# Moving the shared expert's sum, row numbers and a normalization between the engines of a macaron transformer block

## What is computed

```python
# x: (16, 512, 128), 8192 tokens; D = 128, 8 experts of 384, shared expert of 128, 16 heads of 8
def ffn(x):
    normed = (x - mu) * rsqrt(var + eps) * gamma + beta
    probs  = softmax(normed @ router_w.T);  top_v, top_i = top_k(probs, 2);  gates = softmax(top_v)
    out = sum over e of comb[:, e] * swiglu(normed, gate_up_w[e], down_w[e])
    return out + swiglu(normed, shared_gate_up_w, shared_down_w)
x = x + 0.5 * ffn(layernorm(x))
x = x + attention(layernorm(x))        # with relative-position terms
x = x + 0.5 * ffn(layernorm(x))
```

## Time and profile before

| | us |
|---|---|
| median of 3 runs (2189.92 to 2193.46) | 2190.85 |
| profiled execution | 2192.66 |
| its span | 2190.5 |

### The profile page before, as it was taken

How to read it: one execution, slowest core, us unless ns; L and a number is a source line. 1 busy time by engine, 2 the same in 40 slices (tenths; PEclk the granted TensorE clock), 3 DMA queues, 4 the chain that set the end, 5 groups by cost and what they waited for, 6 DMA issues and landing times. The chain is left out here.

```text
span 2190.5 us, 64350 instructions
## 1 busy us (share of the span) xinstructions
PE 2028.2 (93%) x22952; PEld 1233.5 (56%) x22953; DVE 1925.1 (88%) x4201; ACT 1264.3 (58%) x2997; POOL 1258.6 (57%) x1873
## 2 busy tenths in 40 slices
PE   7899999668999999999999999999999877999990
PEld 4589999423444444444444444444444555999990
DVE  6987776596999999999999999999999688877666
ACT  3455555246666666666666666666666344555550
POOL 3777776323555555555555555555555267777650
PEclk8999999899999999999999999999999898999995
DMA  5343222385021012201210110122000134322218
GB/s 163 89 132 84 87 87 66 113 244 144 2 40 40 3 40 41 37 6 40 40 28 15 40 40 11 31 60 40 2 7 7 54 103 126 100 86 86 82 48 234
DMA packets 163707, 147.85 MB, mean 67 GB/s; under 512 B 51858, under 2 KB 138002, under 8 KB 162898
## 3 DMA queue, kind: packets, MB, share of 16 engines
q1 hardware_dynamic: 144288, 108.31, 19.7%
q0 software_dynamic: 17280, 35.56, 4.8%
q10 hardware_dynamic: 1874, 0.51, 0.1%
HBM read 87.81 MB, written 60.45 MB: 68 GB/s over the span
## 5 line engine op out<-in xcount | busy, mean ns | idle before, releaser
L1329 PE MATMUL ps_scores<-c_relw,stat_rel 64*64 64x512 f32 x4096 | 938.6, 597 | 0.0
L1396 ACT ACTIVATE probs<-ps_scores,neg_max 128x512 f32<-128x512 f32 x1024 | 694.9, 683 | 398.2 <-DVE neg_max L1371 397.0
L1371 DVE TENSOR_REDUCE neg_max<-ps_scores 128x1 f32<-128x512 f32 x1024 | 645.1, 663 | 10.6 <-PE ps_scores L1329 9.7
L1364 DVE STREAM_TRANSPOSE probs_T<-probs 128x1024 f32<-128x1024 f32 x512 | 626.9, 1225 | 0.0
L1317 PE MATMUL ps_scores<-keys,stat_keys 64*64 64x512 f32 x2560 | 588.1, 595 | 0.5 <-ACT probs L1396 0.5
L1329 PEld LDWEIGHTS ps_scores<-c_relw,stat_rel 64*64 64x64 f32 x4096 | 279.1, 133 | 278.1 <-issue 209.1
L1317 PE MATMUL ps_scores<-c_batch,stat_keys 64*64 64x512 f32 x1536 | 354.2, 597 | 5.2 <-POOL stat_rel L1264 3.0
L1262 POOL TENSOR_TENSOR stat_keys<-queries_by_head,c_mask 128x128 f32<-128x128 f32 x320 | 152.0, 475 | 312.9 <-PE ps_scores L1329 312.9
L1289 PEld LDWEIGHTS ps_values<-probs_T,values_diag 128*32 128x32 f32 x8192 | 208.2, 109 | 205.3 <-issue 204.0
L1289 PE MATMUL ps_values<-probs_T,values_diag 128*32 128x128 f32 x8192 | 276.1, 276 | 1.1 <-DVE probs_T L1364 1.1
L1317 PEld LDWEIGHTS ps_scores<-keys,stat_keys 64*64 64x64 f32 x2560 | 171.5, 132 | 122.7 <-issue 112.6
(11 more groups left out here) (296 smaller groups left out, 3694.1 us busy)
## 6 DMA issues: line engine op xcount, KB each, us to landing
c_batch<-dispatched SPq DMA_DIRECT2D x142, 129.0 KB
qkv_record<-f1c_rec SPq DMA_DIRECT2D x16, 768.0 KB, 3.9
f1c_Y<-expert_out SPq DMA_DIRECT2D x32, 256.0 KB, 4.3
f2c_Y<-expert_out SPq DMA_DIRECT2D x32, 256.0 KB, 4.0
c_batch<-qkv_record SPq DMA_DIRECT2D x24, 256.0 KB
keys<-qkv_record SPq DMA_DIRECT2D x20, 256.0 KB
attn_out_T<-attn_out SPq DMA_DIRECT2D x16, 256.0 KB, 2.0
c_Os<-attn_out_T SPq DMA_DIRECT2D x16, 256.0 KB, 3.1
```

Source lines behind the costliest of these rows:

```text
L1329: m = nc.tensor.matmul(out, SR[n // 2 % NS][p, h, :, :].rearrange("p h a -> p (h a)"), R[p, w0:w0 + L], start=False, stop=True)
L1364: nc.vector.transpose(PT[G % 2][:, :, 2 * pair:2 * pair + 2, :, :].rearrange("p r i h a -> p r (i h a)"), Pr[U % NPAIR][:].rearrange("p i ...
L1371: nc.vector.reduce_max(nmx[U % NPAIR][:, n % 2:n % 2 + 1], psS[U % NPAIR][:, n % 2, :], AX, negate=True).then_inc(s_mx, 1)
L1396: nc.scalar.activation(Pr[s][:, n % 2, :], psS[s][:, n % 2, :], ACT.Exp, bias=nmx[s][:, n % 2:n % 2 + 1], accum_out=rs[:, G % 2, tt:tt + 1 ...
```

## The change

In the dispatch the shared expert's result is summed by TensorE: `down` adds, after each matmul with the down weights, a matmul of the residual with the identity times two (`twice`) into the same bank, and ACT copies the bank times 0.5 to the residual (`shared` is now ACT's, after the pair's other work; the last stands before `xf` of tile 0). The row numbers are written by ACT as floats (three signals per step, KB), and POOL's copies go, with its wait for the constants, which moves to ACT. An early activation on ACT makes its table load early. PE starts with 22 fillers instead of 16, has six groups of three fillers that follow DVE's statistics and refinement, and the 24 of `wait_busy` go. In f2 the first projection is written to psY, so that the second need not wait for its add. In the combine of f1 ACT normalizes (scale and bias per token group), POOL computes the bias too (four operations instead of two), DVE aggregates before it transposes V, and all of DVE's steps are written out.

```diff
         @block.gpsimd
-            if first:
-                pool.wait_ge(s_w, 16 * NW)
             for p in range(PAIRS):
-                steps = (2 * p, 2 * p + 1)
-                for s in steps:
-                    wait(pool, (s_sc[s % 4], SC * (s // 4)))
-                    for k in range(TOPK):
-                        nc.gpsimd.tensor_copy(n0[k][s % NR][:, :, D].bitcast(U32), tid[:, k, tokens(s)]).then_inc(s_id, 1)
                 wait(pool, (s_E, KE * (p + 1)))
-                for s in steps:
-                    wait(pool, (s_nb, s + 1), (s_id, TOPK * (s + 1)))
+                for s in (2 * p, 2 * p + 1):
+                    wait(pool, (s_nb, KB * (s + 1)), (s_sc[s % 4], SC * (s // 4)))
...
-                tt(residual(s), residual(s), psE[:], ALU.add).then_inc(s_oa, 1)
+                tt(residual(s), residual(s), (psE if s else psY)[:], ALU.add).then_inc(s_oa, 1)
...
-            def shared(s):
-                wait(dve, (s_dn, s + 1))
-                stt(out=residual(s), in0=psY[:], scalar=0.5, in1=residual(s), op0=ALU.mult, op1=ALU.add
-                    ).then_inc(s_add, 1)
...
+                act.wait_ge(s_v, 1)
+                nc.scalar.activation(sh[:, 0:1], zero[:, 0:1], ACT.Identity)
                 act.wait_ge(s_w0, 16 * NW0)
+            nc.scalar.activation(twice[:], ident[:], ACT.Copy, scale=2.0).then_inc(s_tw, 1)
...
             def copy_rows(s):
                 act.wait_ge(s_C, KC * (s + 1))
                 nc.scalar.activation(n0[1][s % NR][:, :, 0:D], n0[0][s % NR][:, :, 0:D], ACT.Copy).then_inc(s_nb, 1)
+                for k in range(TOPK):
+                    nc.scalar.activation(n0[k][s % NR][:, :, D], tid[:, k, tokens(s)], ACT.Copy).then_inc(s_nb, 1)
+
+            def shared(s):
+                wait(act, (s_dn, s + 1))
+                nc.scalar.activation(XR[:, tokens(s), :], psY[:], ACT.Copy, scale=0.5).then_inc(s_add, 1)
...
                 if p == 0:
+                    if first:
+                        act.wait_ge(s_w, 16 * NW)
                     copy_rows(a)
...
+                    shared(a)
                 else:
+                    shared(a - 1)
                     gate(a)
...
                         high(b + 2)
+                    shared(a)
+            shared(NB - 1)
...
-                keep_busy(16)
+                keep_busy(22)
...
             def down(s):
-                wait(pe, (s_h, s + 1), (s_add, s))
+                wait(pe, (s_h, s + 1), (s_add, s), (s_tw, 1))
                 for j in range(JT):
-                    t = nc.tensor.matmul(psY[:, j, :], h[s % 2][:, j * P:(j + 1) * P], sdT[:], start=True, stop=True)
+                    nc.tensor.matmul(psY[:, j, :], h[s % 2][:, j * P:(j + 1) * P], sdT[:], start=True, stop=False)
+                    t = nc.tensor.matmul(psY[:, j, :], twice[:], XR[:, JT * s + j, :], start=False, stop=True)
...
-                for s in range(3):
+                for s in range(2):
                     oproj(s)
+                keep_busy(4)
+                oproj(2)
+            for sem, count in ((s_A, JT), (s_A, 2 * JT), (s_A, 4 * JT), (s_rs, 4), (s_rs, 8), (s_rs, 12)):
+                pe.wait_ge(sem, count)
+                keep_busy(3)
...
                 if p == 0:
-                    wait_busy(p)
                     ranks(p)
```

In `combine`:

```diff
         @block.gpsimd
-                    wait(pool, (s_A, KA * s.n()))
+                    wait(pool, (s_A, KA * s.n()), (s_rs, KN * s.n(-1)))
                     nc.gpsimd.tensor_tensor(ve[:], mv[q][:, :, 1], eps[:], ALU.add).then_inc(s_rs, 1)
-                    wait(pool, (s_rs, 2 * s.n(-1) + 1), (s_C, JT * s.n(-3)))
+                    nc.gpsimd.tensor_scalar(nm[:], mv[q][:, :, 0], -1.0, None, ALU.mult).then_inc(s_rs, 1)
+                    wait(pool, (s_rs, KN * s.n(-1) + 2), (s_C, JT * s.n(-4)))
                     nc.gpsimd.tensor_tensor(rs[q][:], ve[:], mhalf[:], ALU.pow).then_inc(s_rs, 1)
+                    wait(pool, (s_rs, KN * s.n(-1) + 3))
+                    nc.gpsimd.tensor_tensor(sh[q][:], nm[:], rs[q][:], ALU.mult).then_inc(s_rs, 1)
...
         @block.vector
-                    wait(dve, (s_rs, 2 * s.n(-1)), (s_tp, s.n(-3)))
-                    for j in range(JT):
-                        nc.vector.tensor_scalar(xn[s.slot(-2, 2)][:, j, :],
...
-            run_steps(dve, 0, NB + 3, 8, NB, emit)
+            if last:
+                run_steps(dve, 0, NB + 3, 8, NB, emit)
+            else:
+                for n in range(NB + 3):
+                    emit(Step(n // 4, n % 4))
...
         @block.scalar
                     nc.scalar.activation(xT[:], psT[:], ACT.Copy).then_inc(s_xT, 1)
+                if s.on(-1, NB):
+                    q = s.slot(-1)
+                    wait(act, (s_rs, KN * s.n()), (s_tp, s.n(-2)))
+                    for j in range(JT):
+                        nc.scalar.activation(xn[s.slot(-1, 2)][:, j, :], flat(XR[:, bass.ds(JT * s.n(-1) + j, 1), :]),
+                                             ACT.Identity, bias=sh[q][:, j:j + 1], scale=rs[q][:, j:j + 1]).then_inc(s_C, 1)
+                if s.on(-2, NB):
                     q = s.slot(-2)
                     wait(act, (s_r, s.n(-3)), (s_st[q], 16 * s.lap(-2)))
```

More of the change, by code:

```diff
@@ L241, in route @@
         e2 = sb(c, tag + "_e2", [P, NT])
+        twice = sb(c, tag + "_twice", [P, P])
         sh = sb(c, tag + "_sh", [P, NT])
@@ L268, in route @@
                            "rows", "gateup", "silu", "hidden", "down", "added", "whi", "wlo"))
-        s_nb, s_id, s_wd = S("copied"), S("dest"), S("wd")
+        s_nb, s_wd, s_tw = S("copied"), S("wd"), S("twice")
         s_v, s_row, s_x, s_tab, s_G = (S(x) for x in ("map", "padrow", "padded", "tiletab", "gates"))
@@ L287, in route @@
         PAIRS = NB // 2
-        pads = T["pads"].bitcast(F32)
+        pads = T["pads"]
         def tokens(k):
@@ L382, in _ @@
                                                     n0[k][s % NR][:, j, :], None).then_inc(s_sc[s % 4], 16)
-            for q in range(4):
-                pool.wait_ge(s_sc[q], SC * (NB // 4))
             for n in range(ET):
@@ L631, in split @@
                 wait(dve, (s_ld[s.slot(off)], 16 * (s.lap(off) + 1)), (s_st[s.slot(off)], 16 * NS * s.lap(off + 4 - YR)))
-                copy(to[t][:], Xs[s.slot(off, XR8)][:, :, D].bitcast(U32)).then_inc(s_to, 1)
+                copy(to[t][:], Xs[s.slot(off, XR8)][:, :, D]).then_inc(s_to, 1)
             def tile(s):
@@ L637, in tile @@
                     if isinstance(s.i, int) and s.n(-2) == 8:
-                        wait(dve, (s_sc[0], 3 * SC), (s_sc[1], 3 * SC), (s_nb, NB), (s_tp, NB))
+                        wait(dve, (s_sc[0], 3 * SC), (s_sc[1], 3 * SC), (s_nb, KB * NB), (s_tp, NB))
                     if isinstance(s.i, int) and s.n(-2) == 16:
@@ L701, in _ @@
             hidden(1)
-            shared(0)
             for p in range(1, PAIRS):
@@ L710, in _ @@
                 best(p, ch)
-                shared(a - 1)
                 if more:
@@ L721, in _ @@
                     rows(p)
-                    shared(a)
                 else:
@@ L885, in oproj @@
             def oproj(s):
-                wait(pe, (s_os[s % 4], 16 * (s // 4 + 1)), (s_oa, s))
+                wait(pe, (s_os[s % 4], 16 * (s // 4 + 1)), (s_oa, s if s > 1 else 0))
                 for j in range(JT):
-                    t = nc.tensor.matmul(psE[:, j, :], Os[s % 4][:, j * P:(j + 1) * P], wo[:], start=True, stop=True)
+                    t = nc.tensor.matmul((psE if s else psY)[:, j, :], Os[s % 4][:, j * P:(j + 1) * P], wo[:], start=True, stop=True)
                 t.then_inc(s_o, 1)
@@ L1033, in combine @@
             ve = sb(c, tag + "_ve", [P, JT])
+            nm = sb(c, tag + "_nm", [P, JT])
+            sh = [sb(c, f"{tag}_sh{q}", [P, JT]) for q in range(4)]
+            KN = 4
             rs = [sb(c, f"{tag}_rs{q}", [P, JT]) for q in range(4)]
@@ L1126, in emit @@
                     nc.vector.transpose(rc[q][:, 2 * L:3 * L], Vf[q2][:]).then_inc(s_r, 1)
-                if s.on(-1, NB):
-                    for j in range(JT):
-                        nc.vector.bn_aggr(mv[s.slot(-1)][:, j, :], st[:, j, :]).then_inc(s_A, 1)
-            run_steps(dve, 0, NB + 3, 8, NB, emit)
+            if last:
[3 more added lines that the diff above has]
+                    emit(Step(n // 4, n % 4))
         if last:
@@ L1438 @@
         "ones": np.ones((P, P), _F),
-        "tid": np.arange(TOPK * TOK, dtype=np.uint32).reshape(TOPK, NT, P).transpose(2, 0, 1),
-        "pads": np.concatenate([np.zeros((SPARE * P, D), np.uint32),
-                                TOPK * TOK + np.arange(SPARE * P, dtype=np.uint32)[:, None]], axis=1),
+        "tid": np.arange(TOPK * TOK, dtype=_F).reshape(TOPK, NT, P).transpose(2, 0, 1),
+        "pads": np.concatenate([np.zeros((SPARE * P, D), _F),
+                                np.arange(TOPK * TOK, (TOPK * NT + SPARE) * P, dtype=_F)[:, None]], axis=1),
```

19 lines of the change are left out of this document (3 added, 16 removed).

## The result

The changed kernel takes 2206.3 us in the median of 4 runs (2200.6 to 2209.5), the kernel before 2191.2. The ratio is 1.0063, with an interval of 1.0046 to 1.0079: 0.6% slower, where 0.3% faster was forecast and the range ended at 2191. The profiled execution took 2200.64 us with a span of 2198.8. A second set of runs of the same kernel on another chip gave 1.0055 (experiment 9), with a span of 2200.6.

What follows compares the result with a forecast made beforehand. DVE was taken to pace both dispatches, TensorE close behind, and the first combine. Terms -5.5 - 0.7 + 3.9 - 7.5 - 6.6 + 6.5 + 3.3 = -6.6 us took the median from 2190.85 to 2184 us, range 2174 to 2191.

Steps and rivals of the forecast that it cites:

- The start of the first dispatch: Up to the first scatter: early table load, faster logits and transposes, ranks without fillers ahead; 5.5 us sooner.
- the 6.9 us: Gain at the first dispatch's start if the table load also cost the skill page's drain; the forecast took 5.5.
- Start of the second: Second dispatch up to its first scatter: other bank for the projection, full clock, fillers gone; 6.6 us sooner.
- Combine: First layer's combine: 13 steps at 4.85 us through DVE, POOL and ACT; 7.5 us shorter.
- Pairs of the first dispatch: First dispatch's pair loop: DVE relieved, but TensorE's own order becomes the bound; 0.7 us shorter for all pairs.
- First hand-over: First dispatch to experts: ACT's xf queues behind shared, which waits for the longer last down; 3.9 us later.
- one term: Pairs of the second dispatch: the projection comes later without its cover; 6.5 us longer, bounds +2 and +14.
- The second hand-over: Second dispatch to experts: the same wait of xf behind shared, with fewer fillers; 3.3 us later.
- E: Rival: TensorE's sum bounds both dispatches with the clock at its low level; slower, 2198 us; 9%.
- B: Rival: full gain, 2176 us; TensorE never falls to 1.2 GHz and the combine steps in 4.6 us; 20%.
- C: Rival: DMA replaces DVE as the combine's bound at 5.2 us per step; 2188 us; 10%.
- D: Rival: the fillers don't hold the clock, 2.5 + 2.4 us less gained; 2189 us; 12%.

Runs made afterwards that it cites:

- experiment 9: The changed kernel itself, unaltered, timed again on another chip against the kernel before: ratio 1.0055 (1.0042 to 1.0068).
- experiment 7: Changed kernel with ACT's last copy of the shared bank issued behind the first tile's eviction and weight copies; repeated on another chip, ratio 1.0013 to the kernel before.
- experiment 5: Changed kernel with the projection of b+2 issued ahead of down(a-1) in the second dispatch; repeated on another chip, ratio 0.9968 to the kernel before.
- Cheap matmuls (6): Changed kernel with the down step's added matmul a bf16 one of zeros, residual left out; repeated on another chip, ratio 0.9975 to the kernel before.
- more fillers (8): Changed kernel with 12 fillers instead of 4 between gate_up(a) and gate_up(b) in the second dispatch; repeated on another chip, ratio 1.0012 to the kernel before.

## Why the prediction was wrong

**Right, with sizes.** The start of the first dispatch: forecast -5.5, measured -4.4 and -5.5, of which up to 2.7 are given back in the first pair, a step that I had counted at nothing. (The row of the logits in the earlier trace rows holds 13 of their 16 matmuls, in 1.62 us; all 16 took the 1.95 us that I used.) Start of the second: -6.6, measured -6.2. Combine: -7.5, measured -6.7 and -7.5; the chain from GpSimd over ACT to VectorE's transpose, and the 1.5 us for four activations with both operands, were as worked out. Pairs of the first dispatch: -0.7, measured -0.2 and 0.0. First hand-over: +3.9, measured +3.9 and +3.7, and experiment 7 gives 2.5 us of it to ACT's queue. The Trainium skill ("ScalarE: Activation LUTs", What ACT_TABLE_LOAD costs) adds 1380 ns of drain to the load; here the load takes 1.28 us and the activation follows it 0.01 us later (8.21 and 9.50). Between two table sets there is no more: a copy at 122.56 (0.60 us), the load at 123.17, the silu at 124.47. So the trace decides against the 6.9 us that the page would have given.

**Wrong: one term.** "The loop grows by 1.94 us, less some 0.9 us that DVE was behind the logits at full clock: 1 us for 7 pairs", with low-clock stretches on top, gave +6.5 with an upper bound of +14. (Seven times 1.04 us is 7.3 already, so the working didn't give the 6.5 that I took.) It was +16.9 in six pairs, or 2.8 us per pair. I had named the mechanism (the cover gone, the projection 0.97 us later) and mis-sized it in three ways. First, VectorE had no reserve of 0.9 us: in the kernel before it waited for the logits itself in five of the seven pairs (3.6 us, first fence of waits). Its wait for the projection comes early in the pair, ahead of nearly all its work, and what it loses there reaches gate_up(b), the second down step and the next transposes (its add started 4.4 us behind `best` in the pair shown, 1764.94 to 1769.35, and 1.9 us in that of the earlier trace rows, 1794.00 to 1795.89). Second, the down step at the low level is 3.33 us, so the 0.97 becomes 2.36, in a place where nothing covers it; I had priced low stretches once per few pairs, and got two in four of the six. Third, the low clock in the pairs grew from 21 to 34 us, which I hadn't counted; that the longer pairs themselves brought it on is my reading, borne out by experiment 5, where the order alone brought it back to 18.5. Cheap matmuls (6) take 12.9 of the 16.9 away, more fillers (8) 8.4, the order alone (5) 17.0. These overlap and can't be added, since each also shortens what the others shorten.

**The second hand-over** was +3.3 and came out at +5.8 and +4.0; in the first profile its down step fell into a low stretch (1860.5 to 1864).

**The rivals.** E (slower, 2198, 9%) had the right sign and nearly the right profile, with the wrong reason: it wanted TensorE to be the bound of both dispatches, and the first didn't move. What happened is a wait, which two calls in the other order remove. B, C and D didn't occur: the combine wasn't held by DMA (0.79 of share at 234 GB/s, up from 0.73 at 219), and the fillers did hold the clock in the second start. In the first start of the first profile they did so only in part (2.90 us for the logits). The chance of slower, 0.10, was too low: three of my own terms (+3.9, +3.3, +6.5) were all costs of the sum, and I never took them together as a part of the change that has no gain of its own. Forecast of the sum part alone: -0.7 + 3.9 + 6.5 + 3.3 = +13; measured 24 to 34.

## What to carry to other kernels

Before work is moved to an engine with room in its sum, look at what is queued right behind the place where it lands, and who waits for that: the two longer down steps cost 0.4 us per pair with the first behind the projection, and 3.3 us with it ahead (97.8 and 114.8 us against 95.2 without the sum, in six pairs). An idle engine's time is in gaps of a chain; it is only free where the added work lies in a gap. And price each part of a change by itself: here two parts gave 0.9%, and the third took 1.5%.

## What the runs showed of the hardware

The granted clock depended on the order of the work: the same matmuls with the projection first had 18.5 us at the low level in the pairs of the second dispatch, and 33.5 with it behind the down step.

On one of the chips the engines stood in gaps ahead of instructions that waited for nothing that the profile knows (TensorE 9.45 us in one run, 31.09 in another), and all kernels took longer (2451 us for the kernel before, 12% more). The dispatches and the experts took the loss: pairs 1 to 6 of the first dispatch took 152.9 to 163.8 us there, for 87, while the first combine (93.9 to 96.0 us) and attention (1206.0 to 1207.6) were as elsewhere. What the gaps are stays open. A ratio to a kernel timed on that same chip misled all the same (1.0111 there, 1.0012 elsewhere for the same edit), so a chip that is slow as a whole is no place to judge an edit.

Attention took either 1205.9 to 1206.1 or 1207.3 to 1207.6 us in all profiles, whichever parts of the change were in; the 1.6 us that the first profile of the changed kernel seemed to gain there is this.
